# Two column additions of a convolution unit, moved from VectorE to GpSimd

## What is computed

```python
def _L1_conv_ref(x, w1, w3, w5, wd, wf):
    x1 = _conv(x, w1, padding=[(0, 0), (0, 0)])
    x2 = _conv(x, w3, padding=[(1, 1), (1, 1)])
    x3 = _conv(x, w5, padding=[(2, 2), (2, 2)])
    x4 = _conv(x, wd, padding=[(2, 2), (2, 2)], dilation=(2, 2))
    out = jnp.concatenate([x1, x2, x3, x4], axis=1)
    return _conv(out, wf, padding=[(0, 0), (0, 0)])
...
x = x + _L1_conv_ref(_gn(x), L1_conv_w1, L1_conv_w3, L1_conv_w5, L1_conv_wd, L1_conv_wf)
```

## Time and profile before

| | us |
|---|---|
| median of 3 runs | 1895.9 (1895.88 to 1897.46) |
| the profiled execution | 1904.68 |
| its span | 1902.9 |
| busy: TensorE | 1791.7 |
| busy: VectorE | 1474.5 |
| busy: ScalarE | 1032.9 |
| busy: GpSimd | 537.1 |

### The profile page before, as it was taken

How to read it: one execution, slowest core, us unless ns; L and a number is a source line. 1 busy time by engine, 2 the same in 40 slices (tenths; PEclk the granted TensorE clock), 3 DMA queues, 4 the chain that set the end, 5 groups by cost and what they waited for, 6 DMA issues and landing times.

```text
span 1902.9 us, 42762 instructions
## 1 busy us (share of the span) xinstructions
PE 1791.7 (94%) x14516; PEld 1711.8 (90%) x14516; DVE 1474.5 (77%) x1886; ACT 1032.9 (54%) x1736; POOL 537.1 (28%) x315
## 2 busy tenths in 40 slices
PE   4999998999999999899999999989999999989998
PEld 3899978999999997899989998989998999789998
DVE  4777568999786647999968655899987765689997
ACT  0756466555285646554536764745536564665551
POOL 5599800322281000123237000022325400003222
PEclk9999989999999998999999999889999999899999
DMA  7012103666501200556630210256661120035553
GB/s 186 0 39 74 34 16 92 159 167 159 141 4 58 72 2 15 130 156 166 169 87 13 67 53 1 48 145 169 159 158 43 37 71 25 1 92 135 132 134 95
DMA packets 101476, 166.83 MB, mean 88 GB/s; under 512 B 40040, under 2 KB 74568, under 8 KB 101224
## 3 DMA queue, kind: packets, MB, share of 16 engines
q1 hardware_dynamic: 79624, 138.63, 29.1%
q10 hardware_dynamic: 21760, 27.03, 4.4%
HBM read 52.86 MB, written 25.17 MB: 41 GB/s over the span
## 4 chain that ended last, share of the span: by engine, by line
PE 70%; DVE 12%; issue 9%; POOL 2%; ACT 2%; SPq 2%; DMA 2%; DVEq 1%; ACTq 0%; POOLq 0%
PE ps L762 25%; PE ps L646 11%; PE ps L661 7%; PE ps L663 7%; PE ps L662 7%; PE ps L672 6%; PE ps L700 4%; PE ps L620 2%; DVE region L1327 2%; DVE region L1310 2%; DVE region L1219 2%; DVE region L1279 1%; DMA X<-in_x_dram 1%; POOL region L539 1%; DVE region L1230 1%
## 5 line engine op out<-in xcount | busy, mean ns | idle before, releaser
L762 PE MATMUL ps<-region,W 128*96 128x256 f16 (+3 forms) x7316 | 820.8, 272 | 41.4 <-DVE region L1327 18.2
L762 PEld LDWEIGHTS ps<-region,W 128*96 128x96 f16 (+1 forms) x7316 | 798.5, 123 | 61.1 <-DVE region L1327 22.3
L927 ACT ACTIVATE region<-region 96x1056 f16<-96x1056 f32 (+3 forms) x168 | 208.2, 1284 | 296.0 <-DVE region L1226 283.1
L1141 DVE TENSOR_TENSOR region<-V,band 128x2322 f32<-128x2322 f32 x96 | 261.9, 2731 | 125.0 <-PE ps L663 124.1
L549 POOL TENSOR_TENSOR region<-region,X 96x1536 f32<-96x1536 f32 (+1 forms) x44 | 124.1, 2820 | 589.7 <-DVE region L1343 589.7
L559 POOL TENSOR_TENSOR region<-region 96x1056 f32<-96x1056 f32 (+1 forms) x36 | 85.1, 2365 | 684.1 <-ACT region L908 682.8
L1310 DVE SCALAR_TENSOR_TENSOR region<-ps,small,region 96x768 f32<-96x768 f32 (+1 forms) x220 | 204.2, 989 | 50.9 <-ACT region L980 38.3
L661 PE MATMUL ps<-region 128*128 x1152 | 224.1, 276 | 7.3 <-POOL region L539 6.7
L663 PE MATMUL ps<-region 128*128 x1152 | 222.7, 275 | 0.0
L662 PE MATMUL ps<-region 128*128 x1152 | 222.2, 274 | 0.0
L646 PE MATMUL ps<-proj,region 96*128 96x240 f32 x1024 | 214.9, 374 | 0.0
(11 more groups left out here) (167 smaller groups left out, 2043.0 us busy)
## 6 DMA issues: line engine op xcount, KB each, us to landing
region<-region SPq DMA_DIRECT2D x108, 247.5 KB, 3.8
region<-in_x_dram SPq DMA_DIRECT2D x128, 192.0 KB, 2.4
out_dram<-region SPq DMA_DIRECT2D x40, 576.0 KB, 4.2
region<-region ACTq DMA_DIRECT2D x80, 247.5 KB, 2.4
X<-in_x_dram SPq DMA_DIRECT2D x30, 576.0 KB, 6.0
region<-region SPq DMA_DIRECT2D x36, 247.4 KB, 4.9
X<-in_x_dram SPq DMA_DIRECT2D x19, 384.0 KB, 14.9
region<-region SPq DMA_DIRECT2D x24, 185.6 KB, 3.2
```

Of the source, the lines that this page charges most:

```text
L762: last = mm(o, w, src, start=k == 0, stop=k == len(steps) - 1, skip_group_check=split and ck > 0)
L927: act.activation(dst[0:C, a:e, x:z], src, ACT.Copy).then_inc(s_h, 1)
L1141: v.tensor_tensor(T[:, i].rearrange("p m (i j) -> p m i j", j=3), taps.broadcast_to([P, DM, BW // 3, 3]), mask.broadcast_to([P, DM, BW // ...
```

## The change

`outputs` goes from VectorE's program to GpSimd's, word for word but for the engine, and is called at the head of `residual`. Its two waits and its two increments of `s_acc` go with it. The residual addition's own wait for all nine steps stays, and so now waits for GpSimd's own two additions. Everyone else's waits are as they were.

```diff
@@ gpsimd @@
+                def outputs(u, blocks):
+
+                    n = b * UNITS + u
+                    grid = ob.rearrange("p (k i j c) -> p c i k j", i=OR, j=HC, c=2)[:, :, :, 0:blocks]
+                    kind = lambda c: acc[:, :, c, 0:blocks * HC].rearrange("p i (k j) -> p i k j", j=HC)
+                    pool.wait_ge(s_acc, n * NACC + 7 + START)
+                    pool.wait_ge(s_out, n * 16 + START)
+                    for c in range(2):
+                        pool.tensor_tensor(grid[:, c], kind(1 + c), kind(0), ALU.add).then_inc(s_acc, 1)
+
                 def residual(u, r):
 
+                    outputs(u, LASTB if isinstance(u, int) and u == UNITS - 1 else BPU)
                     pool.wait_ge(s_acc, (b * UNITS + u + 1) * NACC + START)
@@ vector @@
-                def outputs(u, blocks):
-
...
                 def window(m, i, k2, whole):
 
                     planes(m + 1, whole)
                     last_rows(m - 1, 1 - i, BPU)
                     lows(m + 1, 1 - i, k2 + i, whole)
-                    outputs(m - 1, BPU)
                     first_rows(m, i, BPU)
...
                 last_rows(UNITS - 2, 1, BPU)
-                outputs(UNITS - 2, BPU)
                 spread_of(st, pst + 4, MEAN, ALU.subtract, NEXT_AT)
...
                 last_rows(UNITS - 1, 0, LASTB)
-                outputs(UNITS - 1, LASTB)
```

## The result

The changed kernel takes 2027.0 us (median of 4 runs, 2026.03 to 2028.55) against 1895.9: 1.069 times as long, 95% interval 1.0672 to 1.0709. So it is 131 us slower; 96 were forecast, with a range that ended at 2022. Of the 131 the two profiled executions show 122.3 (1904.68 and 2027.01). The other 8.8 are what the profiled execution of before lay above its median, and the one of after did not. Of 14 further executions of the kernel before, three took 1902.5 to 1904.6 us with a mean granted TensorE clock of 0.969 of full speed and eleven took 1894.1 to 1899.9 us with 0.972 to 0.975; the profiled one, with 0.968, is like the three.

What follows compares the result with a forecast made beforehand. VectorE's ring was taken as the bound. Per image 7 x 2.65 = 18.6, plus 3.4, 0.9 and 1.05, makes 23.9 us; four images' 95.7 added to the median gives 1991.6; own range 1965 to 2020, 8-in-10 range 1900 to 2022.

Steps and rivals of the forecast that it cites:

- VectorE's ring: VectorE's cycle through one window, 19.59 us, taken as the bound; TensorE's 18.9 us per unit just behind; forecast 22.24 us.
- the pair isn't taken: Rival: a low with float16 second input leaves GpSimd alone in the window, TensorE binds; 1882 us, chance 0.08.
- the price of an addition: One 96 x 768 addition on GpSimd: 1.65 us taken, with 1.54 and 1.82 as ends.
- A turn of an addition: Between the lows, each GpSimd addition holds the shared SBUF port pair and delays VectorE by 1.50 us.
- The residual's turn: The residual addition gets the shared port pair before the fourth low and holds it for 2.75 us.
- the images' ends: After window 8 of each image: 3.4, 0.9 and 1.05 us more.
- The placed parts of unit 9: Low parts placed by DMA, landing at 20.0 us; TensorE stops for them in unit 9, 3.4 us more.
- The group mean's delay: In an image's last unit, 96 x 1 steps meet additions and residual and release the group mean some 0.9 us later.
- The last additions: An image's last unit's additions, about 1.2 us each on GpSimd against 1.43 for both, TensorE waiting: 1.05 us more.
- the tails: Part of the predicted time's own range: the same again as the 10 us from the ends of an addition.
- carrying the sum to the median: The 95.7 us was added to the median of the runs; the profiled execution lay 8.8 us above that median.
- The residual misses its turn: Rival: the fourth low goes first, the residual falls beside `first_rows` at no cost; window 19.56, total 1907 us, chance 0.17.

Runs made afterwards that it cites:

- experiment 1: The changed kernel with GpSimd's residual addition waiting until VectorE's four lows of the same window are done; 1968.0 us, ratio 1.0363.
- experiment 2: The changed kernel with the residual addition as two instructions of half the elements; 1974.3 us, ratio 1.0397.
- experiment 4: The kernel before with one of the two column additions on GpSimd, the other left on VectorE behind the lows; 1926.4 us, ratio 1.0148.
- experiment 5: The changed kernel with the residual left out but for 8 elements and a GpSimd memset of the same tile in its place; 1926.5 us, ratio 1.0146.
- experiment 3: The changed kernel with both additions, and all of GpSimd's work of the window, waiting for the four lows; 1976.7 us, ratio 1.0409.
- experiment 6: The changed kernel with ten spare matmuls on TensorE ahead of its wait for the placed low parts, except in an image's first unit; 2016.1 us, ratio 1.0616.

## Why the prediction was right and where it was wrong

**Right: what bounds, and what the move starts.** VectorE's ring was the bound and became longer; the additions met the lows, the engines took turns instruction by instruction, and the residual came in ahead of the fourth low. The forecast lows were 2.7, 2.1 and 3.6 us; they read 2.89, 2.32 and 3.68, in the order that was forecast, the first two 0.2 us longer. Experiments 1, 2, 4 and 5 each took turns away or shortened one, and the lows followed. The rival "the pair isn't taken", which rested on the lows' float16 input, is out.

**Mis-sized: the price of an addition.** I took 1.65 us between the bounds 1.54 (from the residual's rows) and 1.82 (from the row of `differences`). With no one beside them they take 3.59 us for two back to back, 1814 ns on the mean in experiment 3: the upper bound, which was the row of the instruction that is most like them. The estimate of 1.66 us in the prediction was too low likewise. A turn of an addition so cost VectorE 1.70 and 1.68 us (418.78 to 420.48, and 421.60 to 423.28) and not 1.50, since the instruction is 0.16 longer and only 0.11 to 0.13 us of its start-up are hidden instead of 0.15. The residual's turn came out as forecast, 2.76 against 2.75. The two additions are 0.38 of 22.68 - 22.24 = 0.44; the rest are hundredths in the handovers. Over 28 windows that is 12 us.

**Mis-sized: the images' ends.** From the first low of window 8 to TensorE's first work on the next image the kernel before takes 50.8 us (467.35 to 518.11) and the changed one 59.9 (485.04 to 544.92): 9.1 more, forecast 5.35. In the other three images it is 9.4 to 9.6. The placed parts of unit 9 landed at 20.7 after the low's start and not at 20.0, mostly as the lows were longer: 0.7. TensorE's granted clock fell after its waits, which stood nowhere in the sum: 1.6, the difference to experiment 1 over the same 192 matmuls. The group mean's delay was 1.56 and not 0.9, since the residual held the second small step for its whole length: 0.7. The last additions cost 1.40 and not 1.05: 0.35. That leaves 0.4. Over four images this term is 16 us too small.

**Wrong: carrying the sum to the median.** The two profiled executions, stage by stage:

| stage | before | after | more | forecast |
|---|---|---|---|---|
| up to the first image's window 1 | 330.2 | 326.3 | -3.9 | 0 |
| windows 1 to 8, four images | 549.1 | 635.0 | 85.9 | 74.2 |
| from window 8 to TensorE's first work on the next image, or to the end | 208.6 | 246.2 | 37.6 | 21.4 |
| from TensorE's first work on the next image to its window 1, three times | 815.0 | 817.8 | 2.8 | 0 |
| span | 1902.9 | 2025.3 | 122.3 | 95.7 |

The windows carry 11.7 of the miss and the ends 16.2. The first and the last stage, which the sum leaves alone, come to -1.1 together; that they all but cancel is luck. Adding the sum to the median took it for granted that the changed kernel's profile would lie as far above its median as the one of before did. It did not, and that is the last 8.8 us. The long execution of before goes with the lower granted clock (0.968); whether the clock is the cause is open. The range's upper end held too little: 10 us for the bounds of an addition and the same again for the tails make 2012 and not the 2020 that was written, and there was no term for the clock and none for this. So what failed is the sum's sizes, the addition at 1.65 us (it is 1.81), the image's end at 5.35 us (9.1 to 9.6, with the clock at nothing), and the step from the profiled execution to the median.

**One case was priced wrong without harm.** "The residual misses its turn" was put at 1907 us, with the late residual free of cost. Experiment 1 shows that a late residual pushes `differences`, behind it in the queue, past the moment at which `planes` needs it; there the window is 21.1 us, and 20.7 in the one window of experiment 6 where the residual came late by itself, against 19.56 in the prediction.

## What to carry to other kernels

Before work is moved to GpSimd, list which VectorE instructions with two SBUF inputs will stand beside it: each of GpSimd's reading instructions cost such a neighbour its length here but for some 0.1 us, and so did the work behind the moved part that now starts earlier. The residual, 2.90 us long, cost a window more than either addition; splitting it or placing it beside `first_rows`, whose input is in PSUM, gave 53 and 59 of the 131 us back. A wait on the bounding engine can be what keeps another engine's queue in time; take it away on paper only after following that queue to its end, and keep a term for TensorE's clock wherever the change makes TensorE wait longer (here 1.6 us in 22.4, after a wait of 2.8).

## What the hardware showed beyond the expectation

- Two VectorE instructions that follow each other directly leave room for a waiting GpSimd instruction between them, in every one of the windows; with two GpSimd instructions back to back, VectorE gets in between likewise. Neither engine kept the other out for more than one instruction.
- A GpSimd memset of 96 x 1528 float32 (1.37 us) ran beside a two-input VectorE addition with no effect on it (973 ns on the mean of 40, as without it).
- The additions, which write with a stride of two float32 elements, took GpSimd 1814 ns for 768 elements, as an estimate from `differences` has it (2.13 ns per element and 0.18 us fixed: 1.82 us). Against the residual's rate they took 0.27 us more; whether the stride, the place of the output or the way the inputs lie costs it was not taken apart.
